# A two-layer graph, state-space and expert block: first-stage weights made four tiles ahead, six buffers, new step orders

## The reference, cut to what matters

```python
xn = layernorm(x)
msg = xn @ W + B                                  # 4096 x 256
w = where(adj < 1, exp(-(1/adj - 1)**2 / 0.5), 0) # 4096 x 4096, element by element
x = x + w @ msg
x = x + mamba2(layernorm(x))                      # projection, convolution, chunked state update, gate, norm, projection
```

## Time and profile before

| | us |
|---|---|
| runs | 2406.93, 2407.62, 2405.40 (median 2406.93) |
| profiled execution, its own time | 2406.18 |
| its span | 2404.4 |
| PE busy | 2219.1 (92%) |
| DVE busy | 1828.0 (76%) |
| ACT busy | 1566.5 (65%) |
| POOL busy | 1143.0 (48%) |

### The profile page before, as it was taken

One profiled execution on the slowest core, in us unless ns is written; L12 is line 12 of the kernel. 1 busy time (PEld: TensorE's weight loads), 2 busy tenths in 40 slices (PEclk: granted clock), 3 DMA queues, 4 the chain that ended last, 5 costly groups with the idle time before them and its releaser, 6 DMA issues.

```text
span 2404.4 us, 26210 instructions
## 1 busy us (share of the span) xinstructions
PE 2219.1 (92%) x8900; PEld 1389.7 (58%) x8900; DVE 1828.0 (76%) x2083; ACT 1566.5 (65%) x2533; POOL 1143.0 (48%) x928
## 2 busy tenths in 40 slices
PE   7998999999999999999898999999999997786998
PEld 4443545454545455555766677676666673443886
DVE  5666868676777685422889899898989898896765
ACT  4677677777676765424586767767786767774444
POOL 2101212121222223210988888898888888890000
PEclk9999999999999999999999999999999999898999
DMA  5242333233232323223333233332323321113121
GB/s 213 89 135 97 99 104 105 100 102 106 96 120 82 123 80 132 96 70 125 114 98 115 97 116 103 110 119 90 122 89 123 103 82 36 50 48 114 36 79 44
DMA packets 116311, 238.07 MB, mean 99 GB/s; under 512 B 8226, under 2 KB 65954, under 8 KB 115794
## 3 DMA queue, kind: packets, MB, share of 16 engines
q1 hardware_dynamic: 107106, 204.00, 26.0%
q0 software_dynamic: 8528, 31.36, 3.7%
q10 hardware_dynamic: 544, 1.05, 0.1%
HBM read 216.06 MB, written 20.32 MB: 98 GB/s over the span
## 4 chain that ended last, share of the span: by engine, by line
PE 62%; ACT 11%; POOL 11%; DVE 10%; issue 6%; DMA 0%; DVEq 0%; ACTq 0%; SPq 0%; POOLq 0%
PE ps L674 13%; PE ps L716 9%; POOL dB L2264 6%; PE ps L960 5%; DVE h L1449 2%; PE ps L838 2%; PE ps L812 2%; DVE wgt L1142 2%; POOL acc L2246 2%; PE ps L944 2%; ACT wgt L1634 2%; POOL du L2260 2%; ACT L1632 2%; PE ps L698 2%; PE ps L742 1%
## 5 line engine op out<-in xcount | busy, mean ns | idle before, releaser
L1449 DVE TENSOR_TENSOR_SCAN h<-ps,hst,dB 128x512 f32<-128x512 f32 x512 | 637.8, 1271 | 61.2 <-ACT ps L1634 46.5
L2264 POOL TENSOR_TENSOR dB<-du,bc 128x512 f32<-128x512 f32 x512 | 648.8, 1291 | 61.0 <-DVE h L1449 58.0
L674 PE MATMUL ps<-wgt,msg 128*128 128x512 f32 x1024 | 503.2, 605 | 16.7 <-DVE wgt L1142 15.2
L1634 ACT ACTIVATE ps<-dt,cols 128x512 f32<-128x512 f32 x512 | 350.9, 690 | 181.1 <-DVE h L1449 178.9
L716 PE MATMUL ps<-raw,msg 128*128 128x256 f32 x1792 | 444.9, 383 | 0.9 <-ACT hb L1634 0.9
L960 PE MATMUL ps<-consts,h 128*128 128x128 f32 x2048 | 324.1, 285 | 64.6 <-DVE acc L1420 27.5
L960 PEld LDWEIGHTS ps<-consts,h 128*128 128x128 f32 x2048 | 252.3, 145 | 224.6 <-issue 73.8
L716 PEld LDWEIGHTS ps<-raw,msg 128*128 128x128 f32 x1792 | 327.1, 192 | 83.6 <-issue 51.2
L674 PEld LDWEIGHTS ps<-wgt,msg 128*128 128x128 f32 x1024 | 189.2, 193 | 224.4 <-issue 192.5
L1634 ACT ACTIVATE wgt<-wgt 128x1024 f32<-128x1024 f32 x256 | 258.6, 1047 | 66.6 <-DVE wgt L1135 64.2
L2246 POOL TENSOR_TENSOR acc<-acc,part 128x512 f32<-128x512 f32 x174 | 226.3, 1301 | 59.6 <-ACT part L1634 58.7
(11 more groups left out here) (316 smaller groups left out, 3513.0 us busy)
## 6 DMA issues: line engine op xcount, KB each, us to landing
raw<-in_adjT SPq DMA_DIRECT2D x256, 512.0 KB, 3.6
bc<-tmp_bc SPq DMA_DIRECT2D x64, 512.0 KB, 4.7
E<-tmp_bc POOLq DMA_DIRECT2D x32, 512.0 KB, 4.1
xb<-in_xT POOLq DMA_DIRECT2D x8, 512.0 KB, 4.6
tmp_x<-xb POOLq DMA_DIRECT2D x8, 512.0 KB, 4.8
x<-tmp_x SPq DMA_DIRECT2D x8, 512.0 KB, 4.9
tmp_x<-x SPq DMA_DIRECT2D x8, 512.0 KB, 4.6
raw<-tmp_xn SPq DMA_DIRECT2D x8, 512.0 KB, 4.1
```

Of the source, the lines that this page charges most:

```text
L674: x = e.matmul(P[d][:, :], msg[:, j, d * 128:(d + 1) * 128], wgt[g % NW][:, l, :], start=j == 0, stop=j == NJ - 1)
L1449: e.tensor_tensor_scan(hr[n % 3][:, m, :], PS[4 + k % 2].t[:, :], dBr[k % 4][:, :], hst[:, n % 16, m:m + 1], ALU.mult, ALU.add).then_inc(S ...
L1634: return e.activation(out, in_, func, bias=bias, scale=scale)
L2264: e.tensor_tensor(dBr[k % 4][:, :], du[:, m, :], bcr[i % 3][:, n % 2, :], ALU.mult).then_inc(S("dB"), 1)
```

## The change

The number of wgt buffers goes from 5 to 6, and `prep` is called for tile g + AHEAD with AHEAD = 4 where it was g + 2. In the first pair of messages the "w" steps make tiles 0 to 3 (`chain(prep(0), prep(2))`), in 6 steps from 0.4 on, where 4 steps from 0.6 on made tiles 0 and 1. The tile `th` is gone to make room; lane b of the messages uses `xdecs[1]` for it, which nothing else needs by then. In the blocks' lists the FILLS hold 16 products at eight places where they held 10 at six, the "w" steps run from 0.04 to 0.925 (before: 0 to 0.90), the "pre" steps from 0.005 to 0.95 (before: -0.01 to 0.95), and "evac" is at 0.97 (before: 0.995).

```diff
--- before.py
+++ after.py
@@ -16,7 +16,7 @@
 NJ = N // 128
 NQ = NJ // 2
 NCH = NB * NQ
-NW = 5
+NW, AHEAD = 6, 4
 LAG = 7
 EPS = 1e-5
 TINY = 1e-18
@@ -200,7 +200,6 @@
         rr = sb(cA, "rr", [128, TB])
         xbc = sb(cA, "xbc", [128, 5, TB + 3])
         ccs = [sb(cA, f"cc{i}", [128, 6, TB]) for i in range(2)]
-        th = sb(cA, "th", [128, 2, TB])
         zs = [sb(cA, f"z{i}", [128, 4, TB]) for i in range(2)]
         sms = [sb(cA, f"sm{i}", [128, 4, 32]) for i in range(2)]
         ecd = sb(cA, "ecd", [128, 3, 4, 8])
@@ -267,7 +266,7 @@
 
         spots = [xbs[0][:, :, :], ccs[0][:, 0:2, :]] + [b[:, i:i + 2, :] for b in (*zs, ccs[1]) for i in (0, 2)]
         lane_a = (xc[:, :, :], sq[:, :, :], rr[:, :])
-        lane_b = (ccs[0][:, 2:4, :], ccs[0][:, 4:6, :], th[:, 0, :])
+        lane_b = (ccs[0][:, 2:4, :], ccs[0][:, 4:6, :], xdecs[1][:, :])
 
 
         ring_a, ring_b = Ring(PS[2:5], 6 * NB // 2), Ring(PS[5:8], 6 * NB // 2 + 4)
@@ -355,17 +354,17 @@
 
 
         NP, NPA, NSA, NPB, NPO = 64, 55, 62, 71, 18
-        order_msg = [braid(("a", 9, 0, 1), ("b", 9, 0, 1), ("p", 16, 0, 1) if i else ("w", 4, 0.6, 1)) for i in range(NB // 2)]
+        order_msg = [braid(("a", 9, 0, 1), ("b", 9, 0, 1), ("p", 16, 0, 1) if i else ("w", 6, 0.4, 1)) for i in range(NB // 2)]
         order_first = braid(("pre", NPA, 0, 1), ("p", NP, 0, 0.92))
 
 
-        FILLS, SEND, WFIRST, WLAST, EVAC, PREND = ((4, 2), (7, 2), (38, 1), (50, 2), (55, 1), (58, 2)), 58, 0, 0.90, 0.995, 0.95
+        FILLS, SEND, WFIRST, WLAST, EVAC, PREND = ((5, 3), (7, 2), (8, 2), (25, 2), (30, 2), (38, 2), (50, 2), (57, 1)), 58, 0.04, 0.925, 0.97, 0.95
         order_a = []
         for ib in range(NB):
             ssd_at = spread(NSA, 0, 1)
             at = [(x, "ssd") for x in ssd_at]
             if ib + 1 < NB:
-                at += [(x, "pre") for x in spread(NPA, -0.01, PREND)]
+                at += [(x, "pre") for x in spread(NPA, 0.005, PREND)]
             n_fill = NP if ib + 2 < NB else 24 if ib + 2 == NB else 32
             if ib + 2 < NB:
                 at += [(EVAC, "evac")] + [(x, "w") for x in spread(NP, WFIRST, WLAST)]
@@ -1145,7 +1144,7 @@
             def product_a(ib):
                 for i in range(0, NQ, 2):
                     yield from (None, None, None)
-                    g = ib * NQ + i + 2
+                    g = ib * NQ + i + AHEAD
                     if g < NCH:
                         p = prep(g)
                         yield
@@ -1300,7 +1299,7 @@
                 w.wait_ge(S("rr2"), 2 * ib + 2)
                 e.tensor_tensor(z[:, 0:2, :], z[:, 0:2, :], two(v.ps), ALU.mult).then_inc(v.evac, 1)
 
-            p, first = product_a(0), prep(0)
+            p, first = product_a(0), chain(prep(0), prep(2))
             for i in range(NB // 2):
                 if i == 1:
                     for m in range(4):
```

## The result

The change makes the kernel faster: 2382.44 us, median of 5 runs (2376.08 to 2383.00), against 2406.93 for the kernel before on the same chip (5 runs, 2405.4 to 2408.23). The ratio is 0.9893, 95% interval 0.9882 to 0.9904. The prediction was 2399.3, its range 2385 to 2412: too little gain, and the time lies just under the range. The profiled execution took 2382.66, its span 2380.9.

What follows compares the result with a forecast made beforehand. TensorE was taken to bound blocks ib = 0 to 5 of the first stage. The terms +8.4 - 2.4 - 25.5 + 14.3 + 1.0 - 3.4 = -7.6 us gave 2399.3 us, range 2385 to 2412.

Steps and rivals of the forecast that it cites:

- Opening: First message pairs: VectorE's Q now precedes L1122, +8.4 us; three later pairs lose their mask wait, -2.4 us.
- Head of a block: Start of blocks ib = 0 to 5: 29.7 us of TensorE waits go, 4.2 come back, -25.5 us.
- the dt wait: Start of six blocks: TensorE waits 0.7 us at dt, 4.2 in all; 0.5 by the port rule.
- Tail: End of blocks ib = 0 to 4: new waits of 1.5 (second mean product) and 1.4 us (L850), +14.3 us.
- The low clock: Blocks ib = 0 to 5: 10.2 us of half-clock stretches, likeliest from waits over 2 us; a third goes, -3.4 us.
- Rival (b): Tail of blocks 0 to 4: low clock follows the new waits, so slower, 2411 us; chance 0.18.
- ib = 6 and 7: Last two first-stage blocks: products taken from the thin tail fill other waits in return, +1.0 us.
- LN's wait for a read: ScalarE's LN waits for a nearer read but is ordered behind it by at least one product: 0, at most 1 us.
- Rival (a): End of the blocks: the tail costs nothing, so without its 14.3 us the time is 2385 us; chance 0.22.

Runs made afterwards that it cites:

- `dt_wait`: The kernel after the change with one fill product fewer ahead of the dt product and one more a quarter of a block later; 2390.73 us, ratio 0.9936.
- `mask_late`: The kernel after the change with all "w" steps shifted a little (WLAST 0.935, EVAC 0.9277); 2384.88 us.
- `swap_two`: The kernel after the change with only two of VectorE's mask passes moved by one place, behind the passes TensorE waits for; 2382.68 us.
- `best`: `swap_two` together with an opening that makes tiles 2 and 3 in the second pair of messages; 2376.49 us.
- `best_two`: `best` with one fill product more ahead of the dt product; 2363.21 us, ratio 0.9828.

## Why the prediction was wrong

The places of gain and loss stood, the size and the attribution of one term above all didn't. Against the first stage's measured -29.6 us:

- **Opening: right, a little too cheap.** +8.4 and -2.4, in all +6.0; measured +7.0. L1121 waits behind Q (24.91 for 17.50); the second combining product waits until 38.58 and the third runs at 39.55 (I had said about 38); the first fill product starts at 41.27 for 31.75, +9.5. I had no low clock there: behind TensorE's wait of 7.71 the first two message products start 1.87 us apart at half clock, and VectorE waits for them twice, 2.3 us. Each later pair is 1.0 us shorter (26.53 for 27.55).
- **Head of a block: the waits go, right; the dt wait that was to come back, +4.2, is 0.** Q was indeed stretched by GpSimd, to 3.68 us at 455.50 beside GpSimd's 2.36 at 454.60, but L1189 begins at 460.10 and ends 15.5 us after the mean product's start, as TensorE arrives at dt (14.4 and 15.3 said, and up to 2.5 of disturbance). By the rule cited there (the Trainium skill, "SBUF — State Buffer", "Who interferes with whom") Q would stand still until GpSimd's operation ends at 456.96, 1.46 us; it took 1.32 longer than its 2.36, so the trace agrees with that; the dt wait of 0.5 that I derived from it didn't come. `dt_wait` shows how narrow that is: one product less and it is 0.93. The rows, GpSimd and VectorE:

```profile
454.60 2.36 POOL L2156 TENSOR_TENSOR E<-E,cbm 128x1024 f32<-128x1024 f32 x1 [5.17 <-ACT E L1633]
...
455.50 3.68 DVE L1134 SCALAR_TENSOR_TENSOR wgt<-wgt 128x1024 f32<-128x1024 f32 x2 [2.51 <-ACT wgt L1633]
...
460.10 1.20 DVE L1189 TENSOR_TENSOR xc<-xc,ps 128x1024 f32<-128x1024 f32 x1
```

- **Tail: right in its two places, a quarter too dear:** +14.3 said, 5 x (1.14 + 1.02) = 10.8 measured. At the mean product I had 1.5: 3.8 of VectorE less 2.6 of TensorE, and 0.25 of overlap. The chain took 3.6 (427.02 to 430.63), and the three products end 2.54 after it begins (426.82 + 2.74): 1.07, so the overlap was not to be added. At L849 I had 1.4 (11.8 of VectorE, 10.3 of TensorE); they took 11.6 and 10.6.
- **The low clock: this is the step that failed.** I wrote "Of the 10.2 us of low clock the waits of over 2 us are the likeliest cause, and they go; those of 1.4 and 1.5 us come. I take a third off: -3.4". It measured -15.3. Two things were wrong in it. I counted six short stretches in ib = 0 to 5; there are seven (near 233, 352, 465, 588, 700, 813 and 824 us), as the busy times of ib = 5 in the kernel before would have told, with a clock of 0.97 for its 0.99 elsewhere, and three more in ib = 6 and 7 (932, 1004, 1038), where one is left (971).

```profile
797.00:914.36 117.36, 113.44 (x383) 60.02 (x382) 83.21 (x96) 78.57 (x125) 26.64 (x23) 0.97 0.30 100
```

And I laid all of them to the waits of over 2 us and gave the tail's waits a share. That holds for three of the seven (465, 700, 813), which begin 0.3 to 1.3 us after a wait of 2.0 to 2.2 us ends, and for 1004 and 1038 behind waits of 2.0 and 2.3. The other four and 932 come behind the dt product with its wait of only 0.5 to 0.7 us, a wait that I let stand. One of each kind in the kernel before:

```profile
585.48 1.95 PE L734 MATMUL ps<-Win,xc 128*128 128x8 f32 x16 [0.66 <-DVE xc L1190]
...
700.41 4.54 PE L674 MATMUL ps<-wgt,msg 128*128 128x512 f32 x6 [2.24 <-DVE wgt L1142]
```

Both kinds of wait went, and the tail's waits of 1.0 and 1.1, longer than those at dt, brought no stretch. So nine of ten stretches went: 9 x 1.7 = 15.3 us in place of 3.4, of which 3.4 lie in ib = 6 and 7. (A longer stretch, 6.8 us, follows the first mean product's wait of 4.16 in both kernels.) Rival (b), the slower side, rested on the same mistake.

- **ib = 6 and 7:** +1.0 said, -3.3 measured; without their clock it is +0.1.
- **LN's wait for a read, 0: right for this kernel, wrong as a reason.** I said that its place in the order was behind that read. That holds by the new lists alone; the lead without them costs 150 us of waits on ScalarE.

Rival (a) had 2385, close to what came, but the tail does wait: that the number is near is luck.

The sum with the measured sizes: 7.0 (opening) - 29.7 (head) + 10.8 (tail) - 15.3 (clock) + 0.1 = -27.1. (0.5 of the head stands in ib = 6 and is counted twice.) For the 2.5 us to -29.6 I have an argument and no test: a product behind a wait doesn't overlap the end of the one ahead of it, and TensorE has 12 waits in ib = 0 to 5 where it had 23. The second stage's 6.1 us, for which the forecast had nothing, hid part of the miss: the total fell by 23.5 in the profiled executions, the first stage by 29.6. What isn't settled is why the same wait is followed by a low stretch in three blocks and not in the others. The Trainium skill ("TensorE: Matmul & The Clock Gate", "What's actually happening") says that the monitor of TensorE's activity runs free of the program, which would give such a lottery. The stretches do begin at differing distances behind the dt wait's end, 1.6 to 2.9 us in `mask_late`, `swap_two`, `dt_wait` and `best`, which fits; no run here tests it.

## What to carry to other kernels

Deepening a pipeline moves two limits: the waits for what is made go, and the writer of a buffer comes close behind its last reader. Before crediting a longer lead, lay out the first overwriting pass against the last product that reads the buffer; the order of the steps is part of the change. Where the bound engine is TensorE, price an idle time by where it stands, too: here a short one ahead of a run of small matmuls, where it drew a stretch, cost more in clock than in waiting, and one product moved across it was worth more than both waits of the tail.

## What the runs showed of the hardware

- TensorE's granted clock fell to half for 3.4 us behind a wait of 0.76 or 0.93 us at the dt product in some blocks and not in others of the same execution; ten waits of 1.02 to 1.14 us elsewhere had nothing behind them, and behind waits of 2.0 to 2.3 us away from dt some blocks had a stretch and some not. A stretch in which TensorE was busy throughout cost 1.7 us. Whether the place at dt matters by its small matmuls or by something else there wasn't tested.
- The second stage, the same code in all thirteen kernels profiled, took 1271.7 to 1278.0 us. A gain of under 6 us in the first stage is better read from the trace up to that stage's end than from the total.
- In `best_two`, with TensorE at 0.4 us of idle time a block (109.9 busy in 110.35) and a granted clock of 1.00, VectorE and ScalarE are busy for 84.5 and 83.9: this stage is at its TensorE work, and what is left in it is fewer or cheaper matmuls.
